# Fixed room per expert for the sorted tokens of an attention and mixture-of-experts kernel; two batches' rows sent in earlier stretches, with a seventh low part on VectorE there

## The chip, the cores and the metric

The kernel runs on one core of one Trainium2 chip. The metric is device time of one execution in microseconds (us); lower is better. The profile comes from one execution. Its span runs from the first to the last instruction. The engines are TensorE (PE, with its weight loads as PEld), VectorE (DVE), ScalarE (ACT), GpSimd (POOL) and SyncE (SP, which only issues DMAs here).

## What is computed

The input `x` is 4 batches x 1024 tokens x 128 channels in float32.

```python
x = x + layernorm(attention(layernorm(x)))      # 16 heads of 64
x = x + layernorm(experts(layernorm(x)))        # 8 experts, F = 256, each token takes 2
```

Attention brings its input down to 64 query and 64 key/value channels, brings it up to 16 heads, turns queries and keys by their position, takes softmax(q k / 8) v over all 1024 keys, projects and adds its input. The expert layer takes the two likeliest experts of each token by the router's softmax, weighs them by a softmax over these two probabilities, and sums `(silu(z Wg) * (z Wu)) Wd` over them.

## The kernel before

**Two phases.** Attention works in 32 stretches, `attend(g)` for g = 0 to 31: stretch g takes two heads (a pair) of batch g // 8. Each has 16 steps. In a step TensorE makes two score tiles of 128 keys x 512 queries (L911, L913), ScalarE takes their exponential (L1200), and TensorE multiplies the probabilities of three steps earlier with the values (L932, L934, L936). The probabilities are float32, and TensorE takes them as a high part, read in place as bfloat16, and a **low part** in float16, which VectorE (`low`, L1515) or GpSimd (`low`, L1946) makes by a subtraction, one per step. `DVE_STEPS` says which steps are VectorE's (2, 4, 6, 8, 10, 12); the other ten are GpSimd's. Low part s is made at the start of step s + 1. `LATE_DVE_STEPS` gives VectorE 7, 14 and 16 of them in stretches 29, 30 and 31.

Beside them, stretch g prepares stretches g + 1 (row maxima: `scan`, two matmuls L808 per step, ScalarE's `look_ahead`, VectorE's L1494) and g + 2 (projection and turning: VectorE's `rotate`, a swap of rows by SP's DMAs, GpSimd's `rope_add` L1930 in steps 3, 5, 7, 9), and finishes g - 1. TensorE's side jobs share three PSUM banks in a fixed order, `IN_ORDER`: each job waits, in `free`, until the engine that reads the job three places earlier is done with it.

**Routing.** In stretches 8(n + 1) to 8(n + 1) + 5, batch n's tokens are normalised, split into high and low float16 halves (`low_rows`, L1591, steps 12 and 14 of the sixth) and routed. `rank_tokens` (TensorE, L866 on) counts, for each token and choice, the tokens of the same expert before it; `take_ranks` (VectorE, L1650 to L1654) reads this. For the three early batches that is step 15 of stretches 12, 20 and 28. After the third, `place` (VectorE, L1668 to L1686, step 1 of stretch 29) knows how many units of 256 rows each expert needs and so where each expert's rows begin in a table `slots_in` with room for 31 units; only then are the row numbers `slot_of` complete. `send` (GpSimd, L1981) writes 128 tokens of one choice, 512 bytes each, to their rows by an indirect DMA. There are 48 sends, all behind `placed`: 6 in stretch 29, 21 in stretch 30 and 21 in stretch 31. SP clears `slots_in` by 8 DMAs of 512 KB in stretches 1 to 4 (`clear_slots`).

**Expert phase.** SP waits for all 48 sends, then loads units (`load_unit`, L645). TensorE runs 31 sorted units and then 32 dense ones (the last batch, each quarter with each expert), with `DOWN_LAG` 2. Each sorted unit turns its 256 rows (`turn_unit`, L1004), makes gate and up (`hidden`, L1015) and down (L1041); `store_unit` writes the result to `slots_out`. The column of its expert's weights comes from a register, which `column` (L994) loads for four units at a time. When all is stored, GpSimd gathers the rows back by 48 indirect DMAs (`fetch`, L1986), one after the other, beside the dense units.

```python
LATE_DVE_STEPS = {GROUPS - 3: (2, 4, 6, 8, 10, 13, 15), GROUPS - 2: (0, 1, 2, 3, 5, 6, 7, 8, 9, 11, 12, 13, 14, 15),
                  GROUPS - 1: tuple(range(STEPS))}
RANK_AT, PLACE_AT = (4, 15), (5, 1)
SEND_AT = ([(LAST - 2, s) for s in (11, 12, 13, 14, 15, 15)]
           + [(LAST - 1, s) for s in range(STEPS) for _ in range(2 if s % 3 == 0 and s else 1)]
           + [(LAST, s) for s in range(14) for _ in range(1 + s % 2)])
```

Of the kernel before, what the change touches and what calls it, by code (L numbers as in the profile page):

```python
# [46 lines left out]
COLUMNS = -(-SORTED // 4) * 4  # L47
MOST_UNITS = S * EARLY // UNIT
QUARTERS = S // UNIT
# [28 lines left out]
LATE_DVE_STEPS = {GROUPS - 3: (2, 4, 6, 8, 10, 13, 15), GROUPS - 2: (0, 1, 2, 3, 5, 6, 7, 8, 9, 11, 12, 13, 14, 15),  # L78
                  GROUPS - 1: tuple(range(STEPS))}
# [12 lines left out]
RANK_AT, PLACE_AT = (4, 15), (5, 1)  # L92
# [90 lines left out]
def quarter_before(n, j):  # L183
# [3 lines left out]
    if n == 1 or (n == 2 and j < 2):  # L187
# [7 lines left out]
SEND_AT = ([(LAST - 2, s) for s in (11, 12, 13, 14, 15, 15)]  # L195
           + [(LAST - 1, s) for s in range(STEPS) for _ in range(2 if s % 3 == 0 and s else 1)]
           + [(LAST, s) for s in range(14) for _ in range(1 + s % 2)])
assert len(SEND_AT) == len(SENT)

# [53 lines left out]
def program(nc, x, w_pairs, w_out, w_down, ln_scale, ln_bias, router, w_gate, w_up, w_dn,  # L253
            rope_cos, rope_sin, identity, expert_rows, expert_ids, out):
    with ExitStack() as ctx:
# [82 lines left out]
        slot_base = sb("slot_base", [P, E])  # L338
        base_parts = sb("base_parts", [P, EARLY * CHOICES * TILES, E])
        base_sum = sb("base_sum", [P, EARLY * CHOICES * TILES])  # L340
# [138 lines left out]
        to_clear = [(at, min(clear_rows, SORTED * UNIT - at)) for at in range(0, SORTED * UNIT, clear_rows)]  # L479
# [72 lines left out]
        def unit_rows(rows, unit):  # L552

            return rows[unit * UNIT:(unit + 1) * UNIT, :].rearrange("(i p) d -> p i d", p=P)
# [6 lines left out]
        def _(sp):  # L561
# [75 lines left out]
            def clear_slots(at, n):  # L637
                width = n * 2 * D // P
                sp.dma_start(slots_in[at:at + n, :].rearrange("(p r) d -> p (r d)", p=P),
                             oacc[1][:].bitcast(F16)[:, 0:width]).then_inc(cleared, 16)  # L640
# [39 lines left out]
            for g in range(LAST):  # L680
# [64 lines left out]
        def _(pe):  # L745
# [115 lines left out]
            def rank_tokens(n, dst):  # L861

                pe.wait_ge(route_dve, ROUTE * n + ROUTE)
                own = TILES * E
                for k in range(CHOICES):
                    pe.matmul(dst[:, 0:own], above[:], hots[:, n, k].rearrange("p t e -> p (t e)"), start=k == 0, stop=False,  # L866
# [529 lines left out]
        def _(dve):  # L1396
# [200 lines left out]
            def route(n, part):  # L1597
# [5 lines left out]
                if part == 0:  # L1603
                    dve.wait_ge(logits_ready, n + 1)
                    logits = job_bank("logits", n, 0)[:, 0:TILES * E].rearrange("p (t e) -> p t e", e=E)
                    step(dve.tensor_reduce(lmax[:], logits, AX, ALU.max), 1)
# [37 lines left out]
            def take_ranks(n):  # L1644

                dve.wait_ge(rank_ready, n + 1)
# [4 lines left out]
                dve.tensor_copy(counts[:], src[:, TILES * E:TILES * E + E]).then_inc(rank_steps, 1)  # L1651
                dve.wait_ge(rank_steps, n + 1)
                standing()
                dve.tensor_reduce(ranks[:, n], rank_parts[:], AX, ALU.add).then_inc(ranked, 1)  # L1654
# [3 lines left out]
            def place():  # L1658

                rows = EARLY * CHOICES * TILES  # L1660

                def step(ins, k):
# [6 lines left out]
                                       steps_of[:].unsqueeze(1).to_broadcast([P, E, MOST_UNITS]), ALU.is_gt), 1)  # L1669
                step(dve.tensor_reduce(units_of[:], over_step[:], AX, ALU.add), 2)  # L1670
                step(dve.tensor_tensor_scan(unit_ends[:], units_of[:], zeros[:], 0.0, ALU.add, ALU.add), 3)
                step(dve.tensor_tensor(slot_base[:], unit_ends[:], units_of[:], ALU.subtract), 4)
                step(dve.tensor_scalar(slot_base[:], slot_base[:], float(UNIT), None, ALU.mult), 5)
                own = hots[:, 0:EARLY].rearrange("p b k t e -> p (b k t) e")
# [502 lines left out]
```

## Time and profile before

| | us |
|---|---|
| median of 3 runs | 1509.08 (1507.39 to 1509.79) |
| the profiled execution | 1509.86 |
| its span | 1507.8 |
| stretch 0 begins, 31 ends (ScalarE's first and last exponential) | 58.1, 1312.4 |
| stretches 21, 29, 30, 31 begin | 882.5, 1193.7, 1240.4, 1284.9 |
| last attention matmul begins, first matmul of the expert phase | 1315.0, 1331.3 |

Rows below are of the view that the line above them names. In a row of groups or of the timeline, "out<-in" names the tiles, "xN" counts instructions, and square brackets hold the engine's idle time before it and what ended it. In a window's row stand its length, then busy time and count of PE, PEld, DVE, ACT and POOL, then the granted TensorE clock as a share of full speed (1.00 is 2.4 GHz, 0.50 is 1.2 GHz), the DMA engines' share and GB/s.

### The profile page before, as it was taken

Reading aid. Unit: us, or ns where it says so; the run is one execution under the profiler, and the core shown is the slowest. Engines: PE = TensorE matmul, PEld = TensorE weight load, DVE = VectorE, ACT = ScalarE, POOL = GpSimd, SP = SyncE. Lnnn points to the kernel's source line nnn. Section 1 sums busy time; section 2 is a strip of 40 time slices with the busy share of each in tenths; the row PEclk is TensorE's granted clock in tenths of the full one; section 3 lists DMA queues with packets and bytes.
Section 4 is the critical chain, followed back from the end, with each engine's and each line's share of the span. In section 5 each row is a group of like instructions: output and inputs, shape, how many; then the busy total and the mean of one; then the engine's idle time right before and its main releaser. Section 6 shows DMA issues by size and latency. Waiting matters only on the chain. (4 is left out here: it accounts for less than half of the span.)

```text
span 1507.8 us, 45164 instructions
## 1 busy us (share of the span) xinstructions
PE 1399.6 (93%) x17865; PEld 930.0 (62%) x17865; DVE 1171.5 (78%) x2689; ACT 1066.0 (71%) x2072; POOL 1218.0 (81%) x730
## 2 busy tenths in 40 slices
PE   4899999999999999999999999999999898869995
PEld 1366665666666656666665656666666555659994
DVE  7788887777788788887788788777887888845576
ACT  2677787778877877778788777777877665724344
POOL 5588998888888988989889889899789878825374
PEclk7799999999999999999999999999999999979998
DMA  5444443423232223333333333233232242133222
GB/s 172 116 110 114 114 110 89 110 72 78 65 89 82 72 77 102 79 79 79 90 81 86 79 79 92 75 83 80 76 82 72 58 160 66 46 119 98 68 58 73
DMA packets 101488, 132.87 MB, mean 88 GB/s; under 512 B 16672, under 2 KB 51232, under 8 KB 100896
## 3 DMA queue, kind: packets, MB, share of 16 engines
q1 hardware_dynamic: 98208, 123.70, 30.8%
q0 software_dynamic: 3072, 6.30, 1.5%
q8 instruction: 143, 2.34, 0.7%
q14 instruction: 65, 0.53, 0.1%
HBM read 20.49 MB, written 14.94 MB: 23 GB/s over the span
## 5 line engine op out<-in xcount | busy, mean ns | idle before, releaser
L1200 ACT ACTIVATE probs<-psum 128x512 f32<-128x512 f32 x1024 | 615.1, 604 | 190.7 <-PE psum L913 189.6
L1946 POOL TENSOR_TENSOR probs_lo<-probs 128x1024 f16<-128x1024 f32 x301 | 626.2, 2090 | 113.6 <-ACT probs L1200 112.2
L1494 DVE CUSTOM_DVE_ANT_0 scan_out<-psum,ahead 128x512 f16<-128x512 f32 x512 | 349.4, 686 | 198.1 <-PE psum L808 189.1
L932 PE MATMUL psum<-cv,probs 128*128 128x66 f16 x4096 | 476.8, 193 | 13.3 <-POOL probs_lo L1946 12.8
L934 PE MATMUL psum<-cv,probs 128*128 128x64 f16 x4096 | 476.5, 194 | 0.0
L936 PE MATMUL psum<-cv,probs_lo 128*128 128x66 f16 x4096 | 475.2, 192 | 0.0
L934 PEld LDWEIGHTS psum<-cv,probs 128*128 128x128 bf16 x4096 | 380.6, 97 | 110.7 <-issue 3.1
L932 PEld LDWEIGHTS psum<-cv,probs 128*128 128x128 bf16 x4096 | 385.7, 97 | 74.8 <-POOL probs_lo L1946 12.1
L911 PE MATMUL psum<-q_both,k_twice 128*128 128x512 f16 x1024 | 388.4, 379 | 2.8 <-ACT probs L1200 2.8
L913 PE MATMUL psum<-q_max,k_ones 65*128 65x512 f16 x1024 | 390.9, 382 | 0.0
L936 PEld LDWEIGHTS psum<-cv,probs_lo 128*128 128x128 f16 x4096 | 380.3, 98 | 0.0
L1515 DVE TENSOR_TENSOR probs_lo<-probs 128x1024 f16<-128x1024 f32 x211 | 333.8, 1584 | 0.2
L1182 ACT ACTIVATE ahead<-psum 128x512 f32<-128x512 f32 x512 | 305.9, 597 | 13.8 <-PE psum L808 13.7
L808 PE MATMUL psum<-k_diff,q_lone 128*128 128x512 f16 x512 | 197.9, 386 | 18.7 <-DVE max_all L1494 8.9
L1930 POOL TENSOR_TENSOR rot<-rot,t_swapped 128x512 f32<-128x512 f32 x122 | 168.4, 1381 | 57.8 <-DMA t_swapped<-t_sin 57.5
L808 PE MATMUL psum<-qk_hi,q_lone 128*128 128x512 f16 x512 | 197.4, 386 | 11.2 <-DVE max_all L1494 9.4
L1940 POOL TENSOR_TENSOR qk_lo<-rot,qk_hi 128x1024 f16<-128x1024 f32 x62 | 159.9, 2580 | 0.0
L911 PEld LDWEIGHTS psum<-q_both,k_twice 128*128 128x128 f16 x1024 | 100.4, 98 | 86.6 <-ACT probs L1200 6.1
L913 PEld LDWEIGHTS psum<-q_max,k_ones 65*128 65x128 f16 x1024 | 99.3, 97 | 83.9 <-issue 1.1
L808 PEld LDWEIGHTS psum<-k_diff,q_lone 128*128 128x128 f16 x512 | 50.7, 99 | 93.1 <-DVE max_all L1494 19.5
L1477 DVE TENSOR_TENSOR rot<-psum,cos_sb 128x512 f32<-128x512 f32 x124 | 85.7, 691 | 10.7 <-PE psum L792 3.4
L1291 ACT ACTIVATE act_sb<-psum 128x512 f32<-128x512 f32 x63 | 37.4, 596 | 73.4 <-PE psum L1015 73.0
(219 smaller groups left out, 1898.8 us busy)
## 6 DMA issues: line engine op xcount, KB each, us to landing
t_swapped<-t_sin SPq DMA_DIRECT2D x248, 128.0 KB, 2.0
k_twice<-qk_hi SPq DMA_DIRECT2D x128, 128.0 KB, 2.4
q_lone<-qk_hi SPq DMA_DIRECT2D x64, 128.0 KB, 2.3
q_both<-qk_hi SPq DMA_DIRECT2D x64, 128.0 KB, 2.3
q_both<-qk_lo SPq DMA_DIRECT2D x64, 128.0 KB, 2.4
q_max<-qk_hi SPq DMA_DIRECT2D x64, 128.0 KB, 2.3
k_ones<-qk_lo SPq DMA_DIRECT2D x64, 128.0 KB, 2.4
z_unit<-slots_in SPq DMA_DIRECT2D x31, 128.0 KB, 2.5
```

What stands on the lines that cost most here:

```text
L808: pe.matmul(dst, q_lone[n % 2][a][:, t * P:(t + 1) * P], keys, start=True, stop=True).then_inc(done, 1)
L911: pe.matmul(score_ps[at], k_twice[par][h][:, k0:k0 + P], q_both[par][h][:, qh * HALF:(qh + 1) * HALF], start=True, stop=False)
L913: mm = pe.matmul(score_ps[at], k_ones[h][:, k0:k0 + P], q_max[h][:, qh * HALF:(qh + 1) * HALF], start=False, stop=True)
L932: pe.matmul(acc, high[:, q * P:(q + 1) * P, 1], v[:, 0:VLO], start=opens, stop=False, skip_group_check=True)
L934: pe.matmul(acc[:, 0:DH], high[:, q * P:(q + 1) * P, 1], v[:, VLO:VW], start=False, stop=False, skip_group_check=True)
L936: mm = pe.matmul(acc, probs_lo[t % 4][:, i, q * P:(q + 1) * P], v[:, 0:VLO], start=False, stop=kp == 3 and i == 1, skip_group_check=True)
L1182: act.activation(ahead[m % 2][:], bank[BANK_OF["diff", n, m]], ACT.Relu).then_inc(ahead_done, 1)
L1200: act.activation(probs[s % 4][:, i, :], score_ps[tile % SCORE_BANKS], ACT.Exp, scale=SCALE).then_inc(probs_done, 1)
L1494: dve.tensor_tensor_reduce(scan_out[m % 2][:], bank[BANK_OF["base", n, m]], ahead[m % 2][:], 1.0, LOWEST, ALU.add, ALU.max, max_all[a][:, ...
L1515: dve.tensor_tensor(probs_lo[s % 4][:].rearrange("p a n -> p (a n)"), p, p.bitcast(BF16).rearrange("p (n two) -> p n two", two=2)[:, :, 1] ...
L1930: pool.tensor_tensor(part, part, swap_to(n, j), ALU.subtract).then_inc(rope_sum, 1)
L1946: pool.tensor_tensor(probs_lo[s % 4][:].rearrange("p a n -> p (a n)"), p, p.bitcast(BF16).rearrange("p (n two) -> p n two", two=2)[:, :, 1 ...
```

## The change

**Rooms.** One table `slots` replaces both: each expert has a fixed room of 3072 rows (the most that three batches can send it) and the table 26368 rows of 512 bytes. `rank_tokens` begins with one more matmul that adds the expert's first row to each rank, so `take_ranks` writes `slot_of` itself as soon as its own batch is ranked. `place` no longer makes row numbers for tokens; it makes the first row of each unit, `row_of`. SP reads it into registers, four units per load, ahead of `load_unit` and again ahead of `store_unit`, which writes the result over the unit's own rows. Clearing takes 26 DMAs of 512 KB in stretches 1 to 7, placed among SP's other DMAs.

**Moves.** `take_ranks` goes from step 15 to step 1 of the next stretch, `place` from step 1 to step 15 of stretch 29. 32 sends (batches 0 and 1) go into 13 stretches: steps 5 and 15 in 14, 18, 20, 21, 22, 26, 28, and 5, 7, 15 in 15, 16, 17, 23, 24, 25. In these VectorE also makes low part 14. The 16 sends of batch 2 go into the odd steps of stretches 30 and 31, where VectorE now makes 8 and 12 low parts; stretch 29 has the usual 6. Each send waits for the exponentials of the steps ahead of its own. Gathers wait for dense units, two per unit.

```diff
+MOST_UNITS = S * EARLY // UNIT
+SLOTS = E * MOST_UNITS * UNIT
+ALL_SLOTS = SLOTS + (SORTED - CHOICES * MOST_UNITS) * UNIT
...
+SENDING = (14, 15, 16, 17, 18, 20, 21, 22, 23, 24, 25, 26, 28)
+LATE_DVE_STEPS = {**{g: DVE_STEPS + (14,) for g in SENDING}, GROUPS - 2: (1, 3, 5, 7, 9, 11, 13, 15), GROUPS - 1: (0, 1, 2, 4, 5, 6, 8, 9, 10, 12, 13, 14)}
...
-RANK_AT, PLACE_AT = (4, 15), (5, 1)
+RANK_AT, PLACE_AT = (5, 1), (5, 15)
...
+SEND_AT = [(g, s) for g in SENDING for s in ((5, 7, 15) if g in (15, 16, 17, 23, 24, 25) else (5, 15))]
+SEND_AT += [(g, s) for g in (30, 31) for s in range(1, STEPS, 2)]
...
+            def first_row(unit, regs):
+
+                if unit % IDS_AT_ONCE == 0:
+                    sp.wait_ge(placed, 1)
+                    sp.load(regs, row_of[0:1, unit:unit + IDS_AT_ONCE])
+                return sp.snap(regs[unit % IDS_AT_ONCE], min_val=0, max_val=ALL_SLOTS - UNIT)
...
             def load_unit(unit):
+                first = first_row(unit, rows_from)
                 if unit >= SLOTS_IN:
                     sp.wait_ge(unit_turned, unit - SLOTS_IN + 1)
-                sp.dma_start(z_unit[unit % SLOTS_IN][:], unit_rows(slots_in, unit)).then_inc(unit_in[unit % SLOTS_IN], 16)
+                sp.dma_start(z_unit[unit % SLOTS_IN][:].bitcast(F32), unit_rows(first)).then_inc(unit_in[unit % SLOTS_IN], 16)
...
+                pe.matmul(dst[:, 0:own], ones[:], base_rows[:], start=True, stop=False, skip_group_check=True)
...
                     if (t, k) == (0, 0):
-                        pool.wait_ge(placed, 1)
+                        pool.wait_ge(ranked, n + 1)
                         pool.wait_ge(z_lo_done, CHUNKS * (n + 1))
+                    if 2 * s + i:
+                        pool.wait_ge(probs_done, g * KEY_TILES + 2 * s + i)
                     send(n, t, k)
...
+                beside = FIRST_GATHER + made // 2
+                if made % 2 == 0:
+                    pool.wait_ge(fuse_done, SORTED + beside + 1)
+                else:
+                    pool.wait_ge(added, beside - DOWN_LAG + 1)
                 fetch(j, t, k)
```

**How the order moves.** GpSimd, end of stretch 17 (and of the twelve others), before:

```order
L1946 TENSOR_TENSOR probs_lo<-probs 128x1024
L1955 TENSOR_TENSOR oacc<-oacc,o_part 128x512
L1946 TENSOR_TENSOR probs_lo<-probs 128x1024 x4
```

and of the change (its lines are 22 or 23 further on):

```order
L1969 TENSOR_TENSOR probs_lo<-probs 128x1024
L1978 TENSOR_TENSOR oacc<-oacc,o_part 128x512
L2004 DMA slots<-z_rows,slot_of 26368x128
L1969 TENSOR_TENSOR probs_lo<-probs 128x1024 x3
```

A send stands where GpSimd made low part 14. VectorE at the same place, steps 14 and 15 (the ISA rows are the scans), before:

```order
L1552 BN_STATS ln_st<-res_sb 128x6 x4
L1523 RECIPROCAL o_rden<-psum 128x4
L1525 TENSOR_TENSOR attn<-psum,o_rden 128x4x64
L1494 ISA scan_out,max_all<-psum,ahead 128x512
L1494 ISA max_all 128x1
L1552 BN_STATS ln_st<-res_sb 128x6 x4
```

and of the change:

```order
L1575 BN_STATS ln_st<-res_sb 128x6 x4
L1538 TENSOR_TENSOR probs_lo<-probs 128x1024
L1546 RECIPROCAL o_rden<-psum 128x4
L1548 TENSOR_TENSOR attn<-psum,o_rden 128x4x64
L1517 ISA scan_out,max_all<-psum,ahead 128x512
L1517 ISA max_all 128x1
L1575 BN_STATS ln_st<-res_sb 128x6 x4
```

Low part 14 now stands ahead of step 15's normalising and scan. GpSimd at the end of stretch 31, before:

```order
L1955 TENSOR_TENSOR oacc<-oacc,o_part 128x512
L1981 DMA slots_in<-z_rows,slot_of 7936x256 x18
L1955 TENSOR_TENSOR oacc<-oacc,o_part 128x512
L1981 DMA slots_in<-z_rows,slot_of 7936x256 x6
L1955 TENSOR_TENSOR oacc<-oacc,o_part 128x512
```

and of the change:

```order
L2004 DMA slots<-z_rows,slot_of 26368x128
L1978 TENSOR_TENSOR oacc<-oacc,o_part 128x512
L2004 DMA slots<-z_rows,slot_of 26368x128
L1969 TENSOR_TENSOR probs_lo<-probs 128x1024
L2004 DMA slots<-z_rows,slot_of 26368x128
L1978 TENSOR_TENSOR oacc<-oacc,o_part 128x512
L2004 DMA slots<-z_rows,slot_of 26368x128
L1969 TENSOR_TENSOR probs_lo<-probs 128x1024
```

The run of 24 sends has gone, but the last send and low part 15 now stand behind step 15's exponentials. VectorE where batch 1 is ranked, end of stretch 20, before:

```order
L1525 TENSOR_TENSOR attn<-psum,o_rden 128x4x64
L1494 ISA scan_out,max_all<-psum,ahead 128x512
L1494 ISA max_all 128x1
L1650 TENSOR_TENSOR rank_parts<-psum,hots 128x64 x2
L1651 COPY counts<-psum 128x8
L1414 MEMSET spare 128x1
L1654 TENSOR_REDUCE ranks<-rank_parts 128x16
L1494 ISA scan_out,max_all<-psum,ahead 128x512
```

and of the change, step 1 of stretch 21:

```order
L1524 TENSOR_SCALAR max_turned<-psum 8x128
L1517 ISA scan_out,max_all<-psum,ahead 128x512
L1517 ISA max_all 128x1
L1530 TENSOR_TENSOR aT_lo<-psum,aT_hi 128x512
L1680 TENSOR_TENSOR rank_parts<-psum,hots 128x64 x2
L1681 COPY counts<-psum 128x8
L1437 MEMSET spare 128x1
L1684 TENSOR_REDUCE slot_of<-rank_parts 128x16
L1517 ISA scan_out,max_all<-psum,ahead 128x512
L1517 ISA max_all 128x1
```

Ranking moved behind the attention split (`aT_lo`) of step 1 and ahead of step 2's scan.

## Rows read from the trace of the kernel before

**Rows 1.** Busy time by stretch of time: five engines, granted clock, DMA.

```profile
core 0: us, PE busy (x) PEld busy (x) DVE busy (x) ACT busy (x) POOL busy (x), PEclk, DMA share, GB/s
605.50:1193.70 588.20, 573.62 (x7726) 367.56 (x7724) 471.40 (x1075) 458.25 (x876) 519.56 (x280) 1.00 0.31 80
882.50:920.60 38.10, 36.84 (x506) 23.38 (x505) 31.99 (x65) 29.11 (x57) 32.13 (x18) 1.00 0.33 87
1193.70:1240.40 46.70, 40.05 (x506) 24.83 (x504) 40.52 (x77) 29.13 (x57) 34.30 (x20) 0.93 0.46 145
1240.40:1284.90 44.50, 37.26 (x497) 23.30 (x496) 39.08 (x60) 27.23 (x52) 38.84 (x26) 0.95 0.23 62
1312.40:1331.30 18.90, 2.37 (x73) 2.13 (x70) 2.42 (x6) 1.26 (x1) 13.39 (x13) 0.69 0.18 57
1331.30:1336.60 5.30, 4.46 (x24) 3.27 (x25) 1.37 (x3) 0.60 (x1) 0.00 (x0) 0.50 0.50 145
```

**Rows 2.** Waits: the first in 1193 to 1285 us, the second in the whole span.

```profile
PE psum L932 <- POOL probs_lo L1946: 10.1, 5, 2.7
...
PE psum L866 <- DVE mask_sums L1630: 2.9, 3, 1.0
```

**Rows 3.** Timeline, 1311 to 1332 us: start, length, engine; last, register loads by source line.

```profile
1311.28 1.09 ACT L1200 ACTIVATE probs<-psum 128x512 f32<-128x512 f32 x2 [0.51 <-PE psum L913]
...
1313.03 1.22 DVE L1515 TENSOR_TENSOR probs_lo<-probs 128x1024 f16<-128x1024 f32 x1
...
1315.01 0.20 PE L936 MATMUL psum<-cv,probs_lo 128*128 128x66 f16 x1
...
1326.66 0.96 POOL L1981 DMA_INDIRECT slots_in<-z_rows,slot_of  x1 [0.30 <-issue]
...
1328.93 3.97 SPq L645 DMA_DIRECT2D z_unit<-slots_in  x8
...
1331.32 0.59 PE L1004 MATMUL psum<-ident_half,z_unit 128*128 128x128 f16 x4 [16.12 <-DMA z_unit<-slots_in]
...
L994 PEldq TENSOR_LOAD <-column_of x8: 328/332/518, 1332.5 to 1408.0; - x8
```

**Rows 4.** By source line: ns min/median/max of low parts and of sends.

```profile
L1946 POOL TENSOR_TENSOR probs_lo<-probs x301: 1882/1893/2885, 60.1 to 1277.3; 128x1024 f16<-128x1024 f32 x151
...
L1515 DVE TENSOR_TENSOR probs_lo<-probs x211: 1209/1262/3352, 65.4 to 1313.0; 128x1024 f16<-128x1024 f32 x106
...
L1981 POOL DMA_INDIRECT slots_in<-z_rows,slot_of x48: 954/1432/2027, 1230.2 to 1326.7; - x48
```

**Rows 5.** Timeline of the placement in stretch 29, and a window from 1206.9 us.

```profile
1199.62 0.25 DVE L1668 TENSOR_TENSOR over_step<-counts,steps_of 128x96 f32<-128x96 f32 x1
...
1205.17 0.06 DVE L1686 MEMSET spare<- 128x1 f32 x1
...
1206.04 0.39 PE L808 MATMUL psum<-qk_hi,q_lone 128*128 128x512 f16 x1 [3.77 <-DVE max_all L1494]
...
1206.90:1210.30 3.40, 3.40 (x31) 1.97 (x30) 3.01 (x7) 2.20 (x4) 0.00 (x0) 0.50 0.23 79
```

**Rows 6.** Windows: step 15 of stretch 17, step 15 of stretch 23.

```profile
758.50:760.50 2.00, 2.00 (x31) 1.31 (x30) 1.97 (x9) 1.58 (x3) 2.00 (x2) 1.00 0.12 28
...
994.10:996.20 2.10, 2.10 (x32) 1.34 (x31) 1.15 (x4) 1.62 (x4) 2.10 (x3) 1.00 0.14 31
```

**Rows 7.** Timeline around steps 0 to 2 of stretch 21.

```profile
882.29 0.35 DVE L1650 TENSOR_TENSOR rank_parts<-psum,hots 128x64 f32<-128x64 f32 x2
...
882.76 0.28 DVE L1654 TENSOR_REDUCE ranks<-rank_parts 128x16 f32<-128x128 f32 x1
...
887.34 0.38 PE L808 MATMUL psum<-k_diff,q_lone 128*128 128x512 f16 x1
...
887.74 0.69 DVE L1507 TENSOR_TENSOR aT_lo<-psum,aT_hi 128x512 f16<-128x512 f32 x1 [0.76 <-ACT aT_hi L1188]
```

**Rows 8.** Timeline of GpSimd: the first gather of expert rows.

```profile
1423.56 1.11 POOL L1986 DMA_INDIRECT y_got<-slots_out,slot_of  x1 [18.88 <-DMA slots_out<-y_sb]
```

More of the change, by code:

```diff
@@ L550, in in_dram, with unit_rows @@
             return t[bass.ds(b, 1)].rearrange("b (t p) d -> p (b t) d", p=P)
-        def unit_rows(rows, unit):
-            return rows[unit * UNIT:(unit + 1) * UNIT, :].rearrange("(i p) d -> p i d", p=P)
+        def unit_rows(first):
+            return slots[bass.ds(first, UNIT), :].rearrange("(i p) d -> p i d", p=P)
         def dense(unit):
@@ L864, in rank_tokens @@
                 own = TILES * E
+                pe.matmul(dst[:, 0:own], ones[:], base_rows[:], start=True, stop=False, skip_group_check=True)
                 for k in range(CHOICES):
[L866 removed]
+                    pe.matmul(dst[:, 0:own], above[:], hots[:, n, k].rearrange("p t e -> p (t e)"), start=False, stop=False,
                               skip_group_check=True)
@@ L1650, in take_ranks @@
                     last = dve.tensor_tensor(rank_parts[:, k], before, hots[:, n, k], ALU.mult)
-                dve.tensor_copy(counts[:], src[:, TILES * E:TILES * E + E]).then_inc(rank_steps, 1)
-                dve.wait_ge(rank_steps, n + 1)
+                step(dve.tensor_copy(counts[:], src[:, TILES * E:TILES * E + E]), 1)
                 standing()
-                dve.tensor_reduce(ranks[:, n], rank_parts[:], AX, ALU.add).then_inc(ranked, 1)
+                with nc.allow_low_precision(reason="one of eight parts is not zero, and it is a whole number"):
+                    dve.tensor_reduce(slot_of[:, n], rank_parts[:], AX, ALU.add).then_inc(ranked, 1)
             place_steps = sem("place_steps")
             def place():
-                rows = EARLY * CHOICES * TILES
                 def step(ins, k):
@@ L1683, in place @@
-                step(dve.tensor_tensor(to, base_sum[:, 0:rows], ranks[:, 0:EARLY].rearrange("p b k t -> p (b k t)"),
-                                       ALU.add), 9)
+                step(dve.tensor_tensor(past[:], unit_at[:].unsqueeze(2).to_broadcast([1, COLUMNS, E]),
+                                       unit_ends[0:1, :].unsqueeze(1).to_broadcast([1, COLUMNS, E]), ALU.is_ge), 4)
+                dve.tensor_tensor(jumps[:], past[:], unused[:].unsqueeze(1).to_broadcast([1, COLUMNS, E]), ALU.mult)
@@ L1685, in place @@
+                step(dve.tensor_reduce(expert_of[:], past[:], AX, ALU.add), 5)
+                step(dve.tensor_reduce(jump[:], jumps[:], AX, ALU.add), 6)
+                dve.tensor_scalar(column_of[:], expert_of[:], float(E - 1), float(F), ALU.min, ALU.mult)
+                step(dve.tensor_tensor(row_of[:], jump[:], steps_of[0:1, :], ALU.add), 7)
                 standing()
```

76 lines of the change are left out of this document (37 added, 39 removed).

## Prediction

> **What bounds the kernel now.** I read the busy time by stretch of time first. Over stretches 14 to 28 TensorE is busy 573.6 of 588.2 us at full clock, so it is the bound there and what other engines do costs only what TensorE waits for, 14.6 us in all. The same view shows three places that are not like this [rows 1]. Stretch 29 takes 46.7 us where stretch 21, the same place in the batch before, takes 38.1; stretch 30 takes 44.5 with TensorE busy 37.3; and between 1312.4 and 1331.3 us it does almost nothing. In 29 and 30 the granted clock is 0.93 and 0.95, and VectorE is busy 40.5 and 39.1 us. The waits name two owners: TensorE waits 10.1 us for GpSimd's low parts, which stand behind sends [rows 2], and 3.77 us for a scan behind the 5.6 us of `place` (1199.62 to 1205.23), after which the clock is 0.50 for 3.4 us [rows 5]. The gap between the phases is a chain through GpSimd: its last send starts at 1326.66, SP loads the first unit at 1328.93, and TensorE begins at 1331.32 after 16.12 us idle [rows 3]. The clock is still 0.50 up to 1336.6 [rows 1]. A change of 0.2% is 3.0 us; less than that a measurement can't tell from none.
>
> **The sum**, against the profiled execution's own 1509.86 us (0.8 us over the median of the runs shown).
>
> *The gap between the phases.* The last send now waits for exponential 30 of 32, so for about 1311.9 [rows 3]. Before, 2.27 us lay between the last send's start and the first unit's load, and 2.39 between that and the first matmul [rows 3]. A register load comes in between: TensorE's own took 0.52 at most [rows 3]. 1311.9 + 0.2 (its issue) + 2.27 + 0.52 + 2.39 = 1317.3. On the other side low part 15 goes from VectorE (1.22, begun 1313.03) to GpSimd, behind that send: 1313.1 + 1.9 = 1315.0, against 1314.25, so attention ends at about 1316 instead of 1315.2. The expert phase begins at 1317.3 to 1317.8: -13.8. The 5.3 us at half clock cost 2.65; most of that goes with the long idle. I take -15.5; bounds -10 (sends late by 4 us in a crowded stretch 31) and -16.4.
>
> *Stretches 29 and 30*, 91.2 us. Stretch 29 without sends and with six low parts on VectorE is stretch 21: 38.1. Stretch 30: busy 37.3, of which the 10% of the time at half clock (0.95) are 4.4 us that full clock does in 2.2: 35.1, and 0.4 for the joints. Each odd step now has one send and GpSimd a low part on the even ones, 8 x 1.89 + 8 x 1.7 + two adds of 1.3 = 31 of 35 us, so I count no wait. `place` stays on VectorE and only moves to step 15 of stretch 29; it loses the 128-partition sums and gains `jumps` and `jump`. I price it as before, 3.8 + 1.7 for the half clock. 38.1 + 35.5 + 5.5 = 79.1: -12. Bounds -6 (three of the five waits for low parts stay, 10.1 / 5 = 2.0 us each [rows 2]) and -15 (`place` costs 2).
>
> *The seventh low part.* It takes 1.2 us alone and up to 3.35 when it meets GpSimd's (1209, 1262 and 3352 ns are minimum, median and maximum) [rows 4]. Step 15 lasts 2.0 us. In stretch 17 VectorE is busy 1.97 of it, since statistics lie there; in 23 it has 0.95 free [rows 6]. A scan may come late by about a step, as TensorE shows no wait in either window. So I count 1.0 us for each of the four stretches with statistics (17, 18, 25, 26), a whole low part, 1.2, for 21, where `low_rows` precedes it, 0.8 for 20 and 28, 0.3 for the other six: 8.6 us. Bounds: 0, since step 11 holds the same work (low part, normalising, scan) and all waits of these stretches are 14.6 us, and 22 (1.7 each: a low part of 1.26 and one of 3.35 by turns, less 0.6 of slack).
>
> *Ranking in step 1.* The wait for `mask_sums`, 2.9 us in three, goes [rows 2]. But ranking's bank is that of the `diff` scan of step 2, which must now wait for `take_ranks`. That scan began at 887.34; the attention split ahead of ranking ended at 888.43, and ranking takes 0.75 (882.29 to 883.04), so `ranked` comes at 889.2: 1.9 us late [rows 7]. 3 x 1.9 - 2.9 = +2.8. Bounds -2.9 and +5.7.
>
> *Sends in steps 5 and 7.* 1.43 us and 0.3 of issue each [rows 4]; 13 + 6 of them beside GpSimd's work, while the 13 in step 15 replace a low part of 1.89. GpSimd idles 68.6 us in stretches 14 to 28 [rows 1]; 19 x 1.7 = 32 fit. I take +1.5, bounds 0 and +8: TensorE waits only where several sends follow a backlog.
>
> By the rows, a send that starts while VectorE makes a low part lengthens from 0.954 to as much as 2.027 us [rows 4]. The Trainium skill says otherwise in "SBUF — State Buffer", section "Who interferes with whom": `tensor_tensor` takes only the shared port's read interface and descriptor generation needs the write interface, so the two should not meet. By that rule this term would be 0 and the time 1.5 us less.
>
> *Clears.* 26 DMAs instead of 8, one at a time instead of in twos, all between swaps that have three steps until GpSimd needs them; +0.5, bounds -1 and +4. *Gathers.* The first waits 18.88 us for the last store, up to 1423.56 [rows 8], which is inside the dense units already, and the others follow it; the new waits ask for units that are done by then. 0, within 1.
>
> -15.5 - 12 + 8.6 + 2.8 + 1.5 + 0.5 = -14.1: 1495.8 for a profiled execution, **1495.0 us** for the median.
>
> **The rivals.**
>
> *Cheap low part.* The 13 stretches have the slack that step 11 has, and the send in step 15 relieves GpSimd, which is never idle there. Then low part, sends and clears cost 2 instead of 10.6: 1486. For it: TensorE has no idle time in either window [rows 6]. Against: stretch 17's VectorE has 0.03 us left.
>
> *Gains half lost.* `place` at the end of stretch 29 and ranking each set off a run of late scans, stretch 30 keeps two of its waits, stretch 31's sends end late: -10 - 6 + 13.4 = -2.6, 1506.5. For it: VectorE and GpSimd are both busy 39 of 44.5 us in stretch 30 [rows 1]. Against: with the sends in odd steps no low part stands behind more than one of them.
>
> *The seventh low part throttles TensorE.* VectorE's low part in step 15 meets one of GpSimd's, takes 3.35 us, the scan comes late by over 2 us, and the idle drops the clock as the 3.77 us did: 2.5 + 1.7 in each of 13 stretches is 54.6 instead of 8.6, 1541. It turns the change slower from (27.5 - 4.8) / 13 = 1.75 us per stretch on. Four or five stretches on top of the upper bounds (22 + 5.7 + 8 + 4 = 39.7 against 27.5) give 1515 to 1521. For it: GpSimd is busy all 2.0 us of that step. Against: the waits of 1.0 us for `mask_sums` left the clock at 1.00 all through stretches 14 to 28 [rows 1, 2], and the send takes a low part's place, so that what VectorE meets there is mostly a send, which gives way.
>
> **Chances.** The forecast's own case (1488 to 1504) 0.57, cheap low part 0.22, half lost 0.12, throttled 0.09. Faster by over 0.2%: 0.57 + 0.22 + 0.05 of the half lost = 0.84; within 0.2%: 0.06; slower: 0.09 + 0.01 = 0.10. The range from 1482 to 1507 leaves out the throttled case and a part of the second and third, 0.15 to 0.2.
>
> **What would show it.** The gap ahead of the first unit: 1 to 2.5 us instead of 16.12, with a register load on SP. Stretch 29 about 43 us with `place` at its end, stretch 30 about 36. Stretches 14 to 28: 588.2 + 10, with TensorE's waits for VectorE's scans at the joints of 17, 18, 25, 26 near 1 us. A wait of about 1.9 us on L808's successor in step 2 of stretches 13, 21, 29. From the first unit on nothing but its start differs. It is wrong if stretches 14 to 28 grow by over 25 us, or if any of them shows a clock below 1.00.

## The result and the profile after it

| | before | changed |
|---|---|---|
| median of 15 runs each, one chip, us | 1507.87 | 1515.33 |
| lowest and highest, us | 1504.79, 1511.11 | 1511.83, 1525.44 |
| profiled execution and its span, us | 1509.86, 1507.8 | 1514.05, 1512.3 |

The medians differ by 7.5 us. The ratio of the runs is 1.0058, with a 95% interval from 1.0045 to 1.0071, so 7 to 11 us slower, where the forecast of 1495.0 lay 12.9 below the median of the kernel before and 20.3 below what came. The busy time by stretch of time of the changed kernel, to be read beside [rows 1] (stretches 14 to 28; 29; 30; 31; then step 10 of stretch 15 and what follows it):

```profile
core 0: us, PE busy (x) PEld busy (x) DVE busy (x) ACT busy (x) POOL busy (x), PEclk, DMA share, GB/s
608.30:1214.90 606.60, 578.13 (x7706) 368.83 (x7705) 503.21 (x1083) 459.60 (x877) 539.73 (x298) 0.99 0.31 80
1214.90:1258.00 43.10, 38.28 (x527) 23.83 (x526) 36.66 (x70) 29.42 (x57) 35.37 (x19) 1.00 0.49 153
1258.00:1300.00 42.00, 36.47 (x497) 23.54 (x496) 30.55 (x66) 27.28 (x53) 30.67 (x20) 0.96 0.22 52
1300.00:1331.40 31.40, 27.91 (x465) 19.07 (x464) 29.78 (x31) 22.88 (x44) 21.64 (x14) 1.00 0.09 26
672.70:678.20 5.50, 3.40 (x31) 2.09 (x32) 4.20 (x7) 2.24 (x6) 5.06 (x3) 0.77 0.05 10
675.60:679.00 3.40, 3.40 (x31) 1.95 (x28) 2.32 (x5) 2.07 (x5) 2.16 (x2) 0.50 0.29 64
```

A stretch here runs from the first exponential of its step 0 to that of the next one. By these marks the 4.5 us between the two spans come from (differences are of the unrounded marks):

| part | before | changed | difference |
|---|---|---|---|
| up to stretch 12, stretches 12 and 13 | 605.5 | 608.3 | +2.8 |
| stretches 14 to 28 | 588.2 | 606.6 | +18.4 |
| stretch 29 | 46.7 | 43.1 | -3.5 |
| stretch 30 | 44.5 | 42.0 | -2.5 |
| stretch 31 | 27.4 | 31.4 | +4.0 |
| behind the last exponential | 195.5 | 180.9 | -14.6 |

The last row holds the gap between the phases, and its sum went as forecast. TensorE's wait ahead of the first unit, 16.12 us in [rows 3], is now 1.23 (timeline of the changed kernel, with GpSimd's last send and low part ahead of it):

```profile
1330.10 0.98 POOL L2004 DMA_INDIRECT slots<-z_rows,slot_of  x1 [2.13 <-ACT probs L1223]
1331.51 1.88 POOL L1969 TENSOR_TENSOR probs_lo<-probs 128x1024 f16<-128x1024 f32 x1 [0.43 <-ACT probs L1223]
...
1335.58 0.38 PE L1027 MATMUL psum<-ident_half,z_unit 128*128 128x128 f16 x4 [1.23 <-DMA z_unit<-slots]
```

**Where stretches 14 to 28 lost.** Set step against step, most of the 18.4 us sits in four of 240 steps. Step 10 of stretches 15, 23, 24 and 25 is 3.5, 2.7, 4.1 and 2.7 us longer (with 0.5 in the step behind the first), 13.5 in all; in 16 and 17, which also have a send in step 7, it is not. The waits of stretches 14 to 28, first before, then changed, show who is late:

```profile
PE psum L808 <- DVE max_turned L1501: 1.9, 4, 0.6
```

```profile
PE psum L830 <- DVE max_turned L1524: 11.0, 7, 2.5
```

`max_turned` follows VectorE's `k_diff` (a difference of two tiles in SBUF, 0.69 us when it meets nothing) and its low part. Step 8 to 10 of stretch 15, first the kernel before, GpSimd and then VectorE:

```profile
666.53 1.27 POOL L1930 TENSOR_TENSOR rot<-rot,t_swapped 128x512 f32<-128x512 f32 x1
668.90 2.33 POOL L1946 TENSOR_TENSOR probs_lo<-probs 128x1024 f16<-128x1024 f32 x1 [1.10 <-ACT probs L1200]
...
667.07 1.28 DVE L1486 TENSOR_TENSOR k_diff<-rot 128x512 f16<-128x512 f32 x1
668.27 1.21 DVE L1515 TENSOR_TENSOR probs_lo<-probs 128x1024 f16<-128x1024 f32 x1
669.41 0.27 DVE L1501 TENSOR_SCALAR max_turned<-psum 8x128 f16<-8x128 f32 x1
```

and the changed one, where the send of step 7 ended at 668.0:

```profile
668.02 1.91 POOL L1969 TENSOR_TENSOR probs_lo<-probs 128x1024 f16<-128x1024 f32 x1
669.87 1.28 POOL L1953 TENSOR_TENSOR rot<-rot,t_swapped 128x512 f32<-128x512 f32 x1
671.51 1.95 POOL L1969 TENSOR_TENSOR probs_lo<-probs 128x1024 f16<-128x1024 f32 x1 [0.36 <-ACT probs L1223]
673.43 2.24 POOL L1978 TENSOR_TENSOR oacc<-oacc,o_part 128x512 f32<-128x512 f32 x1
...
669.71 2.00 DVE L1509 TENSOR_TENSOR k_diff<-rot 128x512 f16<-128x512 f32 x1
671.64 2.91 DVE L1538 TENSOR_TENSOR probs_lo<-probs 128x1024 f16<-128x1024 f32 x1
674.47 0.27 DVE L1524 TENSOR_SCALAR max_turned<-psum 8x128 f16<-8x128 f32 x1
...
674.80 0.39 PE L830 MATMUL psum<-k_diff,q_lone 128*128 128x512 f16 x1 [2.19 <-DVE max_turned L1524]
```

Before, GpSimd had 1.10 us to spare ahead of its low part of step 9: `k_diff` ended and VectorE's low part began in that break. Now `k_diff` is still waiting when GpSimd's low part ends at 669.93; GpSimd goes on with its rotation, and `k_diff` ends 0.56 us behind that. The break is 0.36 us, VectorE's low part starts 0.13 us behind GpSimd's and ends 1.09 us behind it, although GpSimd's next operation (`oacc`) follows with no break: here VectorE's got in first, and `oacc` took 2.24 us. TensorE waits 2.19 us and then works 3.4 us at a granted clock of 0.50, its lower level of 1.2 GHz (the two last rows of the busy time above; "half clock" below). That is the kind of idle time that [rows 5] showed behind `place`, in a place where I had looked for none.

**Stretches 29 to 31.** `place` (VectorE, start of stretch 30, with GpSimd's three low parts beside it and TensorE's wait for the scan behind it):

```profile
1258.45 0.25 DVE L1696 TENSOR_TENSOR over_step<-counts,steps_of 128x96 f32<-128x96 f32 x1
1259.03 1.45 DVE L1699 TENSOR_SCALAR unused<-units_of 1x8 f32<-1x8 f32 x1
...
1260.59 2.00 DVE L1701 TENSOR_TENSOR past<-unit_at,unit_ends 1x256 f32<-1x256 f32 x1
1262.62 2.00 DVE L1703 TENSOR_TENSOR jumps<-past,unused 1x256 f32<-1x256 f32 x1
...
1258.47 5.88 POOL L1969 TENSOR_TENSOR probs_lo<-probs 128x1024 f16<-128x1024 f32 x3
...
1266.63 0.61 PE L830 MATMUL psum<-qk_hi,q_lone 128*128 128x512 f16 x1 [5.53 <-DVE max_all L1517]
```

It takes 7.3 us (1258.45 to 1265.8) where it took 5.6 in [rows 5], and TensorE waits 5.53 for 3.77. GpSimd's three low parts follow each other with no break, and `past` and `jumps` each wait for one of them and get in between. In stretch 31 low parts of both engines meet; one of VectorE's took 3.35 us there. Waits of the stretch:

```profile
POOL slots L2004 <- ACT probs L1223: 8.3, 6, 2.5
...
PE psum L955 <- DVE probs_lo L1538: 3.5, 3, 2.0
```

### The profile page after: what moved, and what is told of

The parts are those of the page before. It is cut to its first block and busy times, and to the rows that moved or that the text cites. A ratio compares the mean times of both kernels' runs of the same rounds, so it can differ in the third digit from the quotient of the medians.

```text
span 1512.3 us, 45387 instructions
## 1 busy us (share of the span) xinstructions
PE 1403.6 (93%) x17868; PEld 930.3 (62%) x17868; DVE 1197.5 (79%) x2691; ACT 1068.1 (71%) x2072; POOL 1218.4 (81%) x728
## 3 DMA queue, kind: packets, MB, share of 16 engines
q0 software_dynamic: 3072, 6.30, 1.4%
## 5 line engine op out<-in xcount | busy, mean ns | idle before, releaser
L1538 DVE TENSOR_TENSOR probs_lo<-probs 128x1024 f16<-128x1024 f32 x213 | 348.4, 1637 | 0.3
L830 PE MATMUL psum<-k_diff,q_lone 128*128 128x512 f16 x512 | 197.8, 386 | 34.9 <-DVE max_turned L1524 12.5
L830 PE MATMUL psum<-qk_hi,q_lone 128*128 128x512 f16 x512 | 197.6, 386 | 15.7 <-DVE max_all L1517 11.3
L1953 POOL TENSOR_TENSOR rot<-rot,t_swapped 128x512 f32<-128x512 f32 x122 | 161.4, 1324 | 49.4 <-DMA t_swapped<-t_sin 48.9
L1963 POOL TENSOR_TENSOR qk_lo<-rot,qk_hi 128x1024 f16<-128x1024 f32 x62 | 154.4, 2490 | 0.0
L1199 ACT ACTIVATE qk_hi<-rot 128x512 f16<-128x512 f32 x124 | 80.3, 648 | 10.9 <-POOL rot L1953 10.9
```

The source lines that it names most:

```text
L830: pe.matmul(dst, q_lone[n % 2][a][:, t * P:(t + 1) * P], keys, start=True, stop=True).then_inc(done, 1)
L1538: dve.tensor_tensor(probs_lo[s % 4][:].rearrange("p a n -> p (a n)"), p, p.bitcast(BF16).rearrange("p (n two) -> p n two", two=2)[:, :, 1] ...
L1953: pool.tensor_tensor(part, part, swap_to(n, j), ALU.subtract).then_inc(rope_sum, 1)
```

## The experiments

Twelve kernels ran, four at a time, with the kernel before on the same chip each time. It took 1562.6 us on the chip of the first four and 1507.3 and 1507.2 on the chips of the second and the third four. Of the first chip only lengths of steps are used. The changed kernel itself did not run there, and its four relatives did not come out slower than the kernel before: 1558.9, 1545.4, 1537.6 and 1539.9 us, ratios 0.999, 0.990, 0.985 and 0.987. Behind the last exponential their profiles take 206 to 209 us, where the changed kernel's takes 181. Why, and whether the change is slower on that chip at all, is not shown. The other two chips agree so closely that their runs are compared, by the ratios where it matters; "+2.7" for a step is against that step of the kernel before. All edits are to the changed kernel.

**First theory.** The send of step 7 is the cause, ranking and `place` come on top, and the seventh low part costs nothing. Rival: the terms of the prediction, above all 8.6 us for the seventh low part.

```
-LATE_DVE_STEPS = {**{g: DVE_STEPS + (14,) for g in SENDING}, GROUPS - 2: ...
+LATE_DVE_STEPS = {GROUPS - 2: ...
```

> The changed kernel, with VectorE's seventh low part taken out again: GpSimd makes the low part of step 14 in the thirteen sending stretches. Theory (the loss of stretches 14 to 28 sits in step 10 of stretches 15, 23, 24, 25 and around the ranking, and the seventh low part has cost nothing): within 3 us of the changed kernel, so 1512 to 1518, and steps 10 of those four stretches stay 2.7 to 4.1 us longer than before. Rival (the term of the prediction, 8.6 us for the seventh low part): 1506 to 1508, with the gain spread over steps 14 and 15.

1558.9 us against 1562.6 for the kernel before, and 14 to 21 us over the three other kernels of this chip. The steps decide: 14 and 15 gained nothing, so the rival's gain is nowhere. But my reading fell as well. Step 10 was back to its length of before in all four stretches, and step 4 (with 5) had become 3.8 to 7.2 us longer in 15, 16, 22, 23, 24 and 25.

```
-SEND_AT = [(g, s) for g in SENDING for s in ((5, 7, 15) if g in (15, 16, 17, 23, 24, 25) else (5, 15))]
+SEND_AT = [(g, s) for g in SENDING for s in (5, 15)]
```

> The changed kernel without the six sends in step 7 (six of the 48 sends of rows are left out, the rest keep their steps). Theory (the send of step 7 pushes GpSimd's rotation and low part behind it by about 2 us, into VectorE's difference and low part of step 10, which then take 2.0 to 2.3 and 2.9 us for 1.0 to 1.3 and 1.2, and the scan of step 9's maximum comes late): step 10 of stretches 15, 23, 24, 25 is back at its length of before, 13 us in all, so 1501 to 1504. Rival (those steps are slow by the seventh low part or by the traffic of all sends): 1512 to 1515.

1545.4 us, ratio 0.990. The steps 10 came back (0.0 in all four), but step 4 with 5 of stretches 16, 24 and 25 grew by 6.7, 4.5 and 4.5 us. Half of the theory held: without the send no stall in step 10, but GpSimd then falls behind one stretch later. So the cause is not one send but what GpSimd does around VectorE's low part.

```
-RANK_AT, PLACE_AT = (5, 1), (5, 15)
+RANK_AT, PLACE_AT = (5, 3), (5, 15)
```

> The changed kernel with the ranking of a batch in step 3 of its stretch instead of step 1: no attention turn, projection or turn of maxima shares the banks there. Theory (steps 0 to 2 of stretches 13, 21 and 29 are 2.6, 3.7 and 3.7 us longer than before because the bank of the rank is the one that the scan of step 2 wants, while VectorE takes it only behind the attention's low part): those 10 us come back, and the 1.6 us won in the step 15 ahead of each stay, so 1504 to 1507. Rival (the prediction's single 1.9 us wait in each, the rest is phase or other work): 1508 to 1511.

1537.6 us, ratio 0.985. Steps 1 and 2 of stretches 13, 21 and 29, which are 2.6 to 2.7 us longer in the changed kernel, are as before; steps 3 and 4 are 0.5 longer each against what they were; the 1.6 us won in step 15 of stretches 12, 20 and 28 stay. That gives back 1.3 to 1.7 us in each, under 5 in all and not 10: the 1.0 at the start of stretches 21 and 29 is not the ranking's.

```
-                    if (r, s) == PLACE_AT and n == EARLY - 1:
-                        place()
+                    if (r, s) in PLACE_AT and n == EARLY - 1:
+                        place(PLACE_AT.index((r, s)))
```

(with `PLACE_AT` the steps 0, 2, 4, 6, 8, 10 of stretch 30, and the body cut at its steps)

> The changed kernel with the placing of units cut in six parts, in steps 0, 2, 4, 6, 8, 10 of stretch 30, where VectorE has no low part. Theory (the placing, 7.3 us in one piece at the start of stretch 30, holds up one scan, for which TensorE waits 5.5 us and falls to its lower clock): stretch 30 is 4 to 6 us shorter, 1509 to 1511.5. Rival (VectorE is the bound of stretch 30 in any case, the pieces delay one scan each): within 1.5 us of the changed kernel, 1514 to 1517.

1539.9 us, ratio 0.987. Stretch 30 takes 39.7 us, at full clock, where it took 42.7 to 44.5 in the three runs beside it and 42.0 and 43.4 in the two profiles of the changed kernel: 2.3 to 3.6 us less than the changed kernel's, which is under the 4 to 6 of the theory and over the rival's 1.5 (against its three neighbours it is 3.0 to 4.8). Split, its pieces still hold up one scan (step 5 is 2.9 us longer than before).

**Second theory.** The run with six low parts, taken again below, shows the mechanism at its plainest. Its stretch 16, steps 3 and 4, GpSimd, VectorE and TensorE:

```profile
692.58 3.74 POOL L1969 TENSOR_TENSOR probs_lo<-probs 128x1024 f16<-128x1024 f32 x2
696.28 1.26 POOL L1953 TENSOR_TENSOR rot<-rot,t_swapped 128x512 f32<-128x512 f32 x1
697.51 1.88 POOL L1969 TENSOR_TENSOR probs_lo<-probs 128x1024 f16<-128x1024 f32 x1
699.36 1.25 POOL L1953 TENSOR_TENSOR rot<-rot,t_swapped 128x512 f32<-128x512 f32 x1
700.78 1.78 POOL L2004 DMA_INDIRECT slots<-z_rows,slot_of  x1 [0.16 <-issue]
...
695.48 6.22 DVE L1538 TENSOR_TENSOR probs_lo<-probs 128x1024 f16<-128x1024 f32 x1
...
702.91 0.61 PE L814 MATMUL psum<-c_both,w_hi 128*128 128x512 f16 x1 [4.62 <-DVE max_all L1517]
```

A low part that takes 1.2 us alone takes 6.22: it waits through the rest of one GpSimd operation and three more, and ends 1.09 us behind the last. So GpSimd can go on past a VectorE operation that is already waiting.

It is no rule that VectorE stays out as long as GpSimd makes no break. Over all fourteen profiles a low part of VectorE was waiting 1132 times when a `tensor_tensor` of GpSimd ended and the next followed within 0.1 us. It got in there 1076 times, ending about 1.1 us behind that end, and was passed over 56 times. For `k_diff` it is 76 and 43. In the kernel before (86 such ends, of both operations) and in the last run below, whose sends are late (87), neither was ever passed over; in the changed kernel's profile the low part never was (79), but `k_diff` was 5 of 11 times, in step 8 of stretches 15, 16, 23, 24 and 25. All the cases lie in steps 3, 8 and 9, where GpSimd's rotation follows its low part, and all but three in stretches with early sends. I read it so: sends, or a tenth low part, make GpSimd late, and a stall of TensorE lets it catch up. What makes GpSimd pass in one case and not in the next is not shown.

Then a break that costs GpSimd next to nothing should do more than fewer sends:

```
             def low(g, s):
                 pool.wait_ge(probs_done, g * KEY_TILES + (2 * s + 2))
+                if s in (3, 9) and s - 1 in dve_steps(g):
+                    pool.wait_ge(lo_dve, low_parts_done(g, s - 1)[1])
```

> The changed kernel as it is, as the measure for the runs beside it on this chip, since the chip of the four runs before took 1562.6 us for the kernel before, not 1508. Expected: 0.3 to 0.8% slower than before.

1518.79 us against 1507.33, ratio 1.0069 (1.0056 to 1.0083). Stretches 14 to 28 took 611.6 us, with step 10 of stretch 23 at +8.7. That is a longer wait than in the first profile: `k_diff` takes 8.53 us there for 2.32. It waits through the rest of one GpSimd operation and four more, TensorE waits 7.03 us for 2.48, and 6.8 us at half clock follow where the first profile had none.

```profile
991.13 8.53 DVE L1509 TENSOR_TENSOR k_diff<-rot 128x512 f16<-128x512 f32 x1
...
990.86 1.90 POOL L1969 TENSOR_TENSOR probs_lo<-probs 128x1024 f16<-128x1024 f32 x1
992.71 1.26 POOL L1953 TENSOR_TENSOR rot<-rot,t_swapped 128x512 f32<-128x512 f32 x1
993.93 1.88 POOL L1969 TENSOR_TENSOR probs_lo<-probs 128x1024 f16<-128x1024 f32 x1
995.78 1.25 POOL L1978 TENSOR_TENSOR oacc<-oacc,o_part 128x512 f32<-128x512 f32 x1
997.00 2.11 POOL L1963 TENSOR_TENSOR qk_lo<-rot,qk_hi 128x1024 f16<-128x1024 f32 x1
...
1001.05 0.61 PE L830 MATMUL psum<-k_diff,q_lone 128*128 128x512 f16 x1 [7.03 <-DVE max_turned L1524]
```

The spread of its runs in the first table, 13.6 us against 6.3 for the kernel before, fits such differences.

> The changed kernel, and GpSimd's low parts of steps 3 and 9 wait for VectorE's low part of the step ahead. Theory (VectorE's difference and low part wait as long as GpSimd runs one tensor_tensor behind the other, up to 6.2 us in the run with six low parts; a break in GpSimd's row lets them through): no low part of VectorE over 3.6 us, steps 10 of stretches 15, 23, 24, 25 lose 1 us or less each instead of 2.7 to 4.1, so 8 to 13 us less than the changed kernel. Rival (GpSimd simply has too much work in the stretches with three sends, and the yield only moves the loss to TensorE's wait for GpSimd's low parts): within 3 us of the changed kernel.

1513.91 us, ratio 1.0044 (1.0030 to 1.0057): 4.9 us less than the changed kernel, less than the 8 to 13 expected. The mechanism is as expected for the low part: none over 3.2 us, and steps 10 of the four stretches at +0.9 each. The wait does not guard `k_diff`, which still takes 2.22 us below. Stretch 15, GpSimd and VectorE:

```profile
671.18 1.28 POOL L1953 TENSOR_TENSOR rot<-rot,t_swapped 128x512 f32<-128x512 f32 x1
674.30 1.89 POOL L1971 TENSOR_TENSOR probs_lo<-probs 128x1024 f16<-128x1024 f32 x1 [1.84 <-DVE probs_lo L1538]
...
670.80 2.22 DVE L1509 TENSOR_TENSOR k_diff<-rot 128x512 f16<-128x512 f32 x1
672.94 1.21 DVE L1538 TENSOR_TENSOR probs_lo<-probs 128x1024 f16<-128x1024 f32 x1
...
674.41 0.39 PE L830 MATMUL psum<-k_diff,q_lone 128*128 128x512 f16 x1 [0.71 <-DVE max_turned L1524]
```

What it gives back: about 1 us each at the starts and in step 4 of stretches 16, 24 and 25, where GpSimd is now later, and half clock once at stretches 13 and 14. The rival (GpSimd's work is the bound, and the loss moves) has its part: TensorE's waits for GpSimd's low parts in stretches 14 to 28 rose from 1.8 to 4.5 us.

> The changed kernel with the ranking in step 3, the placing in six parts in stretch 30, all 16 low parts of stretch 31 on VectorE, and no send in step 7: 26 sends in steps 5 and 15, 8 in stretch 30, 14 in steps 0 to 13 of stretch 31. Theory: 10 us from the ranking, 5 from the placing, 4 from stretch 31, and 0 to 13 from step 7 (the run without those sends won them in stretches 15 and 23 and lost others in 16, 24 and 25): 19 to 32 us less than the changed kernel. Rival (GpSimd's work is the bound, so each stall that goes lets it fall behind and stall VectorE elsewhere): 5 to 15 us less.

The edit of `SEND_AT`, beside those above and `GROUPS - 1: tuple(range(STEPS))` for VectorE:

```
+SEND_AT = [(g, s) for g in SENDING for s in (5, 15)]
+SEND_AT += [(30, s) for s in range(1, STEPS, 2)] + [(31, s) for s in range(14)]
```

1504.85 us, ratio 0.9985 (0.9975 to 0.9994): 13.9 less than the changed kernel, which is the rival's 5 to 15. Stretch 31 takes 28.6 us, 30 39.7, 29 39.0; but VectorE's low part of step 2 took 5.47, 4.25 and 5.47 us in stretches 16, 24 and 25, as in the run without the sends of step 7, and 14 to 28 took 608.4.

> The kernel with the ranking in step 3, the placing in six parts, stretch 31 on VectorE and no send in step 7, and in it the two waits of GpSimd for VectorE's low parts. Theory: the stalls of step 4 and step 10 go too, 28 to 34 us less than the changed kernel, and 0 to 12 less than the same kernel without the waits. Rival (the waits cost GpSimd what they save VectorE): the same within 3 us, or slower.

1496.67 us, ratio 0.9930 (0.9916 to 0.9943): 10.7 us faster than the kernel before, 22.1 than the changed one, 8.2 than the same without the two waits. The last is within the 0 to 12 expected, the 22.1 falls short of the 28 to 34. Those 8.2 us are the cleanest measure of what the two waits gain, with what they cost GpSimd taken off. Stretches 14 to 28 take 598.7 us at full clock, and stretches 12 to 31 show no half clock.

```profile
607.30:1206.00 598.70, 575.40 (x7705) 367.77 (x7704) 500.46 (x1083) 458.42 (x876) 528.98 (x292) 1.00 0.31 81
```

**What the single parts are worth.**

> The kernel with the ranking in step 3, the placing in six parts, stretch 31 on VectorE, 26 early sends and GpSimd's two waits (0.993 of before), here with the seventh low part back on GpSimd. Theory (the seventh low part costs only about 1 us at the start of stretches 21, 22 and 29, and without it GpSimd is 1.9 us later in each sending stretch, so its waits in step 3 hold up more): within 4 us of it, 0.991 to 0.996. Rival (the prediction's term, 8.6 us for the seventh low part): 0.987 to 0.989.

1505.02 us, ratio 0.9986 (0.9976 to 0.9995): 8.3 us slower than the same kernel with the seventh low part (on another chip), outside what I expected, and on the other side of the rival. Step 4 is +0.7 to +2.1 in stretches 15, 16 and 21 to 25, where the version with seven has at most +1.0.

> The same kernel (0.993 of before) with the seventh low part, without the waits of the sends for the scores of their step. Theory (these waits, 10.7 us on GpSimd in the changed kernel, delay sends and do not protect anything that TensorE waits for): the same within 3 us, 0.991 to 0.995. Rival (without them the sends come ahead of low parts that TensorE is waiting for): over 5 us slower.

1499.61 us, ratio 0.9949 (0.9937 to 0.9962), 2.9 more than with the sends' waits for the exponentials and within what I expected; the intervals overlap, so whether these waits help stays open. Time moves between two stretches: 29 takes 42.9 us and 30 takes 34.9, for 39.0 and 39.7.

> The changed kernel without the seventh low part once more, for the chip on which the changed kernel took 1518.8 us. Theory (GpSimd is later by a low part, and its unbroken row of rotation and low parts covers VectorE's low part of step 3 in five to six stretches, as the earlier profile of this kernel shows with 4.1 to 6.2 us for it): 10 to 30 us slower than the changed kernel, 1525 to 1545, if that chip comes up, and no part of it in steps 14 and 15. Rival (the prediction's term): 1510.

1532.21 us, ratio 1.0173 (1.0158 to 1.0187), 13.4 over the changed kernel of the second chip (15.7 by the ratios), since this run fell on the third: the seventh low part on VectorE is a gain, not a cost. Four low parts take 4.0 to 6.2 us (stretches 15, 16, 22, 25, step 4 with 5 at +3.8 to +7.3), and this time step 10 of stretches 23 and 24 stalls too (+9.1, with a `k_diff` of 8.54 us, and +4.2), where the same kernel on the first chip had stalled in their steps 4. Where the stall falls is a matter of who is late; that it falls somewhere is not.

> The changed kernel with its one table of rooms, its ranking and placing, but all 48 sends where the kernel before has them, in stretches 29 to 31, with its low parts and without the new waits of the sends. Theory: stretches 14 to 28 are back at 588 us (up to 1 more), the gap between the phases is back at 14 to 16 us and stretches 29 to 31 at 118 to 124, so 1508 to 1515. Rival (the new table and its clears have a price or a gain of their own over 3 us): outside that range, with the difference in stretches 1 to 12 or behind the gap.

1508.75 us, ratio 1.0010 (1.0002 to 1.0019). Rooms, clears, ranking and placing alone cost 1.6 us (0.3 to 2.9 by the interval); stretches 29 to 31 take 115.8 us, 2 less than I expected. The gap is back (197.1 us behind the last exponential), and stretches 14 to 28 are back too, but for 0.2 us. So the early sends, with the low part that goes with them, are what adds 18 us there and takes 15 to 16 us off the gap:

```profile
608.40:1196.80 588.40, 573.59 (x7706) 367.20 (x7704) 472.55 (x1072) 458.71 (x876) 517.84 (x279) 1.00 0.31 79
```

## Why the prediction was wrong

The forecast was -14.1 and the spans differ by +4.5: 18.6 us apart. With each term put where its work lies (ranking's 1.9 for stretch 29 there), 8 of them are in stretches 14 to 28 (+18.4 where "588.2 + 10" stood), 4 in 29 and 30, 4 in 31, 1 in the gap and 1 ahead of stretch 14. By the prediction's own steps, with the changed kernel's profile beside it:

- *The gap between the phases*, -15.5: right in its sum, -14.6, and the wait of 1.23 us lies in the 1 to 2.5 named. Its parts were off. From the last exponential to the first unit's matmul it is 4.2 us for 18.9, -14.8 where I had -13.8; the 1.7 for the clock did not come, since from that matmul to the end it is 176.7 us for 176.5. I also misread when the last send may start: exponential 30 ends at 1310.77, where the row of 31 and 32 in [rows 3] has its 0.51 us of idle time, and not at 1311.9.
- *Ranking in step 1*, +2.8: right. The run with the sends left late shows it alone: steps 1 and 2 of stretches 13, 21 and 29 are +2.6, +2.7, +2.7 (less 0.4 in step 4 of the first), steps 15 ahead of them -1.6, -1.6, -1.7, +2.7 in all. Both sides were larger than 1.9 and 1.0, by the same amount.
- *Stretches 29 and 30*, -12: -6.0, or -8.7 without ranking's 2.7 in stretch 29. For 29 I took stretch 21 of before, but 21 itself is 3.7 us longer now, and 29 as well: 43.1 for 38.1, of which 2.7 are ranking's, 1.0 the start named below, and 1.3 no run explains. In 30 `place` was priced at 5.5; it keeps TensorE waiting 5.53 and costs 1.7 more at half clock, and the low parts beside it make `unused`, `past` and `jumps` 1.45, 2.00 and 2.00 us. Without the one-piece `place` stretch 30 is 39.7, not 35.5; only the run whose sends do not wait for exponentials has 34.9, with 3.9 us more in stretch 29.
- *Stretch 31* had no term at all, and cost 4.0. VectorE lost four low parts there, but of the twelve left two waited for one of GpSimd's (2.92 and 3.35 us). With all sixteen on VectorE, and the sends of that stretch in steps 0 to 13, it takes 28.6. I had looked at it only for when the last send ends.
- *The seventh low part*, +8.6 (0 to 22): the sign is wrong. Its own cost is there, at the starts of stretches 21, 22, 23 and 15 (1.0, 1.4, 0.4, 0.5) and 29 (1.0), as these vanish in the runs with six. But it takes a low part off GpSimd, and without it the kernel is 13 to 16 us slower, and 8 in the version with the two waits. I priced what VectorE pays and not what GpSimd is spared.
- *Sends in steps 5 and 7*, +1.5 (0 to 8): this is the step that failed most: it put what the sends make others wait for at next to nothing, and step 10 alone cost 13.5 us. It rested on "GpSimd idles 68.6 us in stretches 14 to 28; 19 x 1.7 = 32 fit". They fit, and TensorE waits for GpSimd's low parts as little as forecast: 1.8 us, as before. What I missed is that GpSimd's lateness is paid by VectorE: in step 8 to 10 its `k_diff` and low part now meet GpSimd's operations, where before they met the end of one and a break of 1.10 us. The prediction had the row for it, low parts from 1209 to 3352 ns [rows 4], and used it for step 15 only. Nor is 3.35 us a limit: a low part took 6.22 and `k_diff` 8.53 us where GpSimd passed over them.

The rival *the seventh low part throttles TensorE* gave 1515 to 1521 for its weaker form, and the time fell there, with late scans and half clock as it described. Its mechanism was a low part of VectorE that meets one of GpSimd's; its place (step 15) and its culprit (the seventh) were wrong. Its signs "over 25 us" and "a clock below 1.00" in stretches 14 to 28: the first stayed at 18.4, the second came true twice, 0.96 in stretches 15 and 24.

The other 4.9 of the 18.4 us are ranking's -0.6 and 5.5 in pieces of up to 1.4 us: 3.3 at the starts named above, the rest under 1 us each. What makes stretches 15, 23, 24 and 25 stall and 16 and 17 not is a matter of tenths (in 17 the send of step 7 took 0.98 us and not 1.97, in 16 GpSimd still had a break of 0.88), and no run tried it by itself.

## What to carry to other kernels

Work added to GpSimd can fit and still cost: once GpSimd was late, VectorE's two-input operations met its `tensor_tensor` operations and waited for one of them, or for up to five. So ask of added work there not only whether it fits but whose operation lay in the gap. A wait that makes GpSimd give way at the two places where VectorE is on the path gained 8.2 us at no change of the work (4.9 in the changed kernel). Before pricing a move of work from one engine to another, price the engine that is relieved too.

## What the runs showed of the hardware

- VectorE's 128x1024 low part took 1.2 us with GpSimd idle, 2.91 behind one GpSimd `tensor_tensor`, and 6.22 behind the rest of one and three more; the 128x512 `k_diff` took 0.69 alone and 8.53 behind the rest of one and four more. The Trainium skill has in "SBUF — State Buffer", section "Who interferes with whom", that a VectorE instruction with two SBUF inputs contends with a GpSimd one that reads SBUF and that the first to issue blocks the other for its whole instruction. The trace agrees: with the next of GpSimd's right behind, the waiting one got in at the end of that instruction in 1072 of 1107 cases (low parts, all profiles) and in 69 of 97 (`k_diff`). That it can be passed over by up to four more that come later is more than the section says.
- A small operation waits as a large one does: `past`, one partition of 256, took 2.00 us in the changed kernel behind a low part of GpSimd, and 0.41 in the fastest version:

```profile
1261.82 0.41 DVE L1704 TENSOR_TENSOR past<-unit_at,unit_ends 1x256 f32<-1x256 f32 x1
```

- A send that starts while VectorE makes a low part takes longer. In the changed kernel 29 sends did, and 26 of them took over 1.1 us (the other three met its last 0.15 us); of the 19 others 18 took less. Before, 28 of 28 took over 1.1 us and 18 of the 20 others less. The low parts beside sends alone took 1.2 us as ever, so there the send gives way. The line of the sends (min, median, max ns) against 954/1432/2027 in [rows 4]:

```profile
L2004 POOL DMA_INDIRECT slots<-z_rows,slot_of x48: 960/1781/2212, 621.7 to 1330.1; - x48
```

  The Trainium skill's rule in the same section, marked there as inferred, that `tensor_tensor` and descriptor generation don't meet, does not hold by these counts; the measurement decides.
- Ahead of step 10 TensorE waited 2.2 to 2.5 us 13 times in five profiles; 3 of these waits were followed by no half clock and 10 by 3.4 us of it. Waits of 7.0 us were followed by 6.8 us of it four times and by 10.2 once. The same wait of 2.48 us in stretch 25 cost 2.7 us in one profile of the changed kernel and 4.2 in the other.
